# Softmax division in PSUM before a three-pass output projection, expert outputs scattered per tile, layer norms scaled on ScalarE

## What is computed

```python
x = layernorm(x + ttt(x))          # L0: chunked test-time-training "attention", 8 chunks of 256
x = layernorm(x + relu_moe(x))     # L0: router, top-1 of 8 experts with a capacity, 128->512->128
x = layernorm(x + attention(x))    # L1: 16 heads of 64, softmax(Q K^T / 8) V, then Wo and a bias
x = layernorm(x + gated_moe(x))    # L1: gate sigmoid(top logit), 8 experts 128->352->128, and a shared one
```

## Time and profile before

| | us |
|---|---|
| median of 3 runs (lowest, highest) | 1915.83 (1913.63, 1916.16) |
| the profiled execution's own time | 1917.79 |
| its span in the profile | 1916.5 |
| PE busy of the span | 1685.4 (88%) |
| VectorE busy | 1327.3 (69%) |
| POOL busy | 1286.8 (67%) |
| ScalarE busy | 787.4 (41%) |

### The profile page before, as it was taken

How to read it: one execution, slowest core, us unless ns; L and a number is a source line. 1 busy time by engine, 2 the same in 40 slices (tenths; PEclk the granted TensorE clock), 3 DMA queues, 4 the chain that set the end, 5 groups by cost and what they waited for, 6 DMA issues and landing times.

```text
span 1916.5 us, 34532 instructions
## 1 busy us (share of the span) xinstructions
PE 1685.4 (88%) x13785; PEld 986.1 (51%) x13785; DVE 1327.3 (69%) x2083; ACT 787.4 (41%) x1183; POOL 1286.8 (67%) x652
## 2 busy tenths in 40 slices
PE   4988851848999999999999999999999999995793
PEld 3766641825555555555555555555555545442483
DVE  3566545666777777777777777777777788764575
ACT  3455430523444444444444444444444444442221
POOL 2233303135988888888888888888888889894303
PEclk8677755969999999999999999999999999997797
DMA  7000000210000000000000000000000000002112
GB/s 237 3 3 3 4 1 20 62 28 1 1 1 1 1 1 1 1 1 1 1 1 1 1 1 1 1 1 1 1 1 1 1 1 1 1 1 81 49 42 61
DMA packets 35190, 29.70 MB, mean 15 GB/s; under 512 B 4060, under 2 KB 30928, under 8 KB 35032
## 3 DMA queue, kind: packets, MB, share of 16 engines
q1 hardware_dynamic: 27064, 20.28, 3.5%
q0 software_dynamic: 2048, 4.20, 0.7%
q10 hardware_dynamic: 5920, 3.01, 0.5%
HBM read 18.31 MB, written 9.18 MB: 14 GB/s over the span
## 4 chain that ended last, share of the span: by engine, by line
PE 68%; DVE 8%; issue 6%; POOL 3%; DMA 1%; ACT 1%; DVEq 0%; POOLq 0%
PE psum L1799 22%; PE psum L1784 16%; PE psum L1759 9%; PE psum L1781 6%; DVE a_On L1994 3%; DVE a_mx L1962 3%; PE psum L1431 2%; PE psum L1813 2%; PE psum L1807 2%; PE psum L1732 1%; PE psum L1392 1%; PE psum L1207 1%; PE psum L1219 1%; PE psum L1441 1%; PE psum L1733 1%
## 5 line engine op out<-in xcount | busy, mean ns | idle before, releaser
L2075 POOL TENSOR_TENSOR a_acc<-a_acc,a_Pb 128x1024 f32<-128x1024 f32 x448 | 1066.0, 2379 | 147.0 <-ACT a_Pb L1899 102.0
L1962 DVE TENSOR_REDUCE a_mx<-psum 128x2 f32<-128x1024 f32 x512 | 624.9, 1223 | 274.7 <-PE psum L1759 274.2
L1899 ACT ACTIVATE a_Pb<-psum 128x1024 f32<-128x1024 f32 x512 | 498.1, 1024 | 646.5 <-PE psum L1784 646.5
L1799 PE MATMUL psum<-a_Pb,a_Vb 128*64 128x512 f32 x2048 | 494.1, 603 | 0.0
L1799 PEld LDWEIGHTS psum<-a_Pb,a_Vb 128*64 128x64 f32 x2048 | 127.0, 136 | 242.5 <-issue 171.8
L1759 PE MATMUL psum<-a_Kh,a_Qh 64*128 64x512 f32 x1024 | 237.3, 457 | 15.5 <-DVE a_mx L1962 15.0
L1759 PEld LDWEIGHTS psum<-a_Kh,a_Qh 64*128 64x128 f32 x1024 | 99.2, 184 | 251.9 <-issue 243.2
L1781 PE MATMUL psum<-a_Mr,a_ones_r 64*128 64x512 f32 x1024 | 203.8, 393 | 0.0
L1784 PE MATMUL psum<-a_Qh,a_Kh 64*128 64x512 f32 x1024 | 202.9, 391 | 0.0
L1784 PE MATMUL psum<-a_Ql,a_Kh 64*128 64x512 f32 x1024 | 202.8, 391 | 0.0
L1784 PE MATMUL psum<-a_Qh,a_Kl 64*128 64x512 f32 x1024 | 202.3, 389 | 0.0
(11 more groups left out here) (372 smaller groups left out, 1905.1 us busy)
## 6 DMA issues: line engine op xcount, KB each, us to landing
x_rows<-zero ACTq DMA_DIRECT2D x2, 1472.0 KB, 15.7
g_w<-in_L_ffn_w_eDF_dram SPq DMA_DIRECT2D x2, 1408.0 KB, 8.8
r_W<-in_L_ffn_W_dram SPq DMA_DIRECT2D x1, 2048.0 KB, 11.5
r_tile_x<-x_rows SPq DMA_DIRECT2D x23, 64.0 KB, 1.9
y_rows<-r_tile_y SPq DMA_DIRECT2D x23, 64.0 KB, 1.5
g_tile_x<-x_rows SPq DMA_DIRECT2D x23, 64.0 KB, 1.9
y_rows<-g_tile_y SPq DMA_DIRECT2D x23, 64.0 KB, 1.5
g_w<-in_L_ffn_w_eFD_dram SPq DMA_DIRECT2D x2, 512.0 KB, 10.8
```

The source lines that it names most:

```text
L1799: last = pe.matmul(ps[HEAD[h], B_O, :], b.Vb[:, p // 2 % 2, kc, at], b.Pb[:, step % BUFS, h * QT:(h + 1) * QT], start=(kc == 0), stop=(kc ...
L1899: act.activation(b.Pb[:, step % BUFS, :], ps[:, slot:slot + 2, :].rearrange("p a b -> p (a b)"), ACT.Exp, scale=SCALE).then_inc(S["probs"], 1)
L1962: v.tensor_reduce(b.mx[:, :, qc, quarter:quarter + 1], ps[:, bank:bank + 2, :], AX.X, ALU.max).then_inc(S[f"free{bank}"], 1)
L2075: g.tensor_tensor(b.acc[:, u, :], before, b.Pb[:, step % BUFS, :], ALU.add).then_inc(S["added"], 1)
```

## The change

It has five parts. (1) The division by the row sums happens in place in PSUM: two reciprocals each in rounds 2 and 3, one 128x512 multiply at the end of round 3; then ScalarE writes the rounded high part and VectorE in round 4 the low part, and the projection runs as three rounded passes like the others. `Wo` gets high and low parts (a fourth ScalarE copy and a fourth POOL subtraction ahead of the first expert layer). The output job moves from round 2 of the unit after next to round 5 of the next unit, the values job from round 3 to round 6; the mask product uses rounded operands. (2) Rows of `x_rows` get a 129th word, the token's number (a spare row's number where no token is). POOL scatters each finished tile straight to the tokens' rows of `y_rows`; four plain loads on SP replace the 16 gathers. The load of tile t+5 now waits for the scatter of tile t to have landed, since the words lie in the loaded tile; there are five buffers. (3) The norms' scaling is four ScalarE activations per group, with VectorE's work on the next group written ahead. (4) The zero fill's source is a memset of 23 rows per partition, made by POOL after its constants; loads of attention weights wait for the fill. (5) The second router's product waits for all five small loads of its layer instead of one.

```diff
+    pool.did(g.iota(k.i32[3][:, :], pattern=[[P, NT + SLOTS_T]], base=0, channel_multiplier=1))
+    g.tensor_copy(k.x_pad[:, :, P:P + 1].bitcast(I32), k.i32[3][:, 0:NT].unsqueeze(2)).then_inc(S["const"], 1)
+    pool.did(g.memset(rows, 0.0))
+    g.tensor_copy(rows[:, :, P:P + 1].bitcast(I32), k.i32[3][:, NT:].unsqueeze(2)).then_inc(S["const"], 1)
...
-    a.wait_ge(S["const"], 1)
+    a.wait_ge(S["const"], 2)
...
+    def scales(g):
+        v.wait_ge(S["deviations"], 4 * stage + g + 1)
+        dve.did(v.reciprocal(k.sd[:, at], k.sd[:, at]))
+        v.scalar_tensor_tensor(k.shift[:, at], k.mv[:, at, 0:1].rearrange("p a b -> p (a b)"), -1.0, k.sd[:, at],
+                               ALU.mult, ALU.mult).then_inc(S["norm_scales"], 1)
+    for g in range(4):
+        moments(g)
+        if g:
+            scales(g - 1)
+    scales(3)
...
+        for i in range(g * GROUP, (g + 1) * GROUP):
+            last = act.activation(k.x_all[:, i, :], k.y_all[:, i, :], ACT.Identity, bias=k.shift[:, i:i + 1], scale=k.sd[:, i:i + 1])
...
+def tile_rows_back_pool(k, r, b):
+    for t in range(SLOTS_T):
+        u = t % BUFS_T
+        g.wait_ge(S["tile_yt"], SLOTS_T * r + t + 1)
+        g.wait_ge(S[f"tile_x{u}"], 16 * tile_uses(r, t))
+        place = b.xt[:, u, P:P + 1].bitcast(U32)
+        g.indirect_dma_start(k.y_rows[r], bass.IndirectOffsetOnAxis(place, 0), b.yt[:, u, :], None).then_inc(S[f"tile_y{u}"], 16)
+def outputs_sp(k, r, got):
+    stores_done(sp, k, r)
+    for g in range(4):
+        rows = k.y_rows[r][at.start * P:at.stop * P, :].rearrange("(a p) d -> p a d", p=P)
+        sp.dma_start(got[:, at, 0:P], rows).then_inc(S[f"tokens_out{g}"], 16)
...
-BUFS_T = 4
+BUFS_T = 5
...
-        sp.wait_ge(S["tile_in"], SLOTS_T * r + t - BUFS_T + 1)
+        sp.wait_ge(S[f"tile_y{u}"], 16 * (tile_uses(r, t) - 1))
...
-    if d == 2 and U > 1:
-        return "out", U - 2
-    if d == 3 and p // 2 < PAIRS // 2 - 1:
-        return "v", p // 2 + 1, U % RN
     if d == 4 and U < UNITS - 2:
         return "q", U + 2
+    if d == 5 and U:
+        return "out", U - 1
+    if d == 6 and p // 2 < PAIRS // 2 - 1:
+        return "v", p // 2 + 1, U % RN
...
+        pe.matmul(ps[:, bank, :], hi, b.Onh[:, :], start=True, stop=False)
+        pe.matmul(ps[:, bank, :], lo, b.Onh[:, :], start=False, stop=False)
+        end(pe.matmul(ps[:, bank, :], hi, b.Onl[:, :], start=False, stop=True), bank)
...
-        if U and 2 <= d <= 5:
-            invert(U - 1, d - 2)
+        if U and d in (2, 3):
+            for part in (2 * d - 4, 2 * d - 3):
+                invert(U - 1, part)
+        if U and d == 4:
+            normalised_low(U - 1)
         if early:
             maximum(*early[1:])
...
-        if U and d in (3, 5, 6, 7):
-            normalise(U - 1, (3, 5, 6, 7).index(d))
+        if U and d == 3:
+            normalise(U - 1)
```

More of the change, by code:

```diff
@@ L841, in ttt_pool, with norms_dve @@
         residual(c)
-def norm_dve(k, n, g, have_stats=False):
+def norms_dve(k, stage, residual=None):
     S, v, dve = k.S, k.nc.vector, k.dve
-    tiles, at = range(g * GROUP, (g + 1) * GROUP), slice(g * GROUP, (g + 1) * GROUP)
-    if not have_stats:
-        for i in tiles:
[L850 to L860, removed]
@@ L863, in norm_act, with moments @@
-def norm_act(k, n, g):
-    S, act = k.S, k.nc.scalar
-    at = slice(g * GROUP, (g + 1) * GROUP)
-    act.wait_ge(S["variances"], n + 1)
-    act.activation(k.sd[:, at], k.mv[:, at, 1:2].rearrange("p a b -> p (a b)"), ACT.Sqrt, bias=k.eps[:, 1:2]).then_inc(S["deviations"], 1)
+    def moments(g):
+        tiles = range(g * GROUP, (g + 1) * GROUP)
+        if residual:
+            residual(g)
+            for i in tiles:
+                dve.did(v.bn_stats(k.stats[:, i, :], k.y_all[:, i, :]))
+        dve.wait()
+        for i in tiles:
+            last = v.bn_aggr(k.mv[:, i, :], k.stats[:, i, :])
+        last.then_inc(S["variances"], 1)
@@ L1226, in relu_act @@
     b, S, ps, act = k.r, k.S, k.ps, k.nc.scalar
-    for g in range(4):
-        norm_act(k, g, g)
+    norms_act(k, 0)
     transpose_route_act(k, 0, b.route_xT)
@@ L1253, in relu_dve @@
     b, S, ps, v, dve = k.r, k.S, k.ps, k.nc.vector, k.dve
-    for g in range(4):
-        norm_dve(k, g, g, True)
+    norms_dve(k, 0)
     v.wait_ge(S["relu_turned"], 1)
@@ L1329 @@
 QT = 512
-GW_LOADS = (1, 4, 5)
+GW_SHARED, GW_ROUTED = 5, 5
 def allocate_gated(k, mem):
@@ L1638, in __init__ @@
                 self.job(misc_job(R), B_P)
-        for key in (("out", UNITS - 2), ("sum", UNITS - 1), ("out", UNITS - 1)):
+        for key in (("sum", UNITS - 1), ("out", UNITS - 1)):
             self.job(key, B_P)
@@ L1810, in output @@
     def output(U):
-        pe.wait_ge(S["normalised"], 4 * U + 4)
+        freed(("sum", U))
         bank = begin(("out", U))
-        end(pe.matmul(ps[:, bank, :], k.att_o[:, U // NU, :], b.On[:, :], start=True, stop=True), bank)
+        hi, lo = (w[:, U // NU * P:(U // NU + 1) * P] for w in k.att_o)
+        pe.matmul(ps[:, bank, :], hi, b.Onh[:, :], start=True, stop=False)
+        pe.matmul(ps[:, bank, :], lo, b.Onh[:, :], start=False, stop=False)
+        end(pe.matmul(ps[:, bank, :], hi, b.Onl[:, :], start=False, stop=True), bank)
     def misc(key):
@@ L1855, in attention_pe @@
     weigh(ROUNDS - 1)
-    output(UNITS - 2)
     sums(UNITS - 1)
@@ L1925, in attention_act @@
             {"q": queries, "k": keys, "v": values}[key[0]](*key[1:])
-        if key and key[0] == "sum":
-            sums(U - 1)
         if d == 0 and U:
             heads_out(U - 1)
+        if d == 3 and U:
+            normalised(U - 1)
     heads_out(UNITS - 1)
-    sums(UNITS - 1)
-    for g in range(4):
-        norm_act(k, 8 + g, g)
+    normalised(UNITS - 1)
+    norms_act(k, 2)
 def attention_dve(k):
@@ L2052, in attention_norm_dve, with residual @@
     S, ps, v, dve = k.S, k.ps, k.nc.vector, k.dve
-    for g in range(NU):
+    def residual(g):
         at = slice(GROUP * g, GROUP * g + GROUP)
```

178 lines of the change are left out of this document (95 added, 83 removed).

## The result

The changed kernel takes **1891.76 us** in the median of four runs (1887.10 to 1896.85), the kernel before 1915.99 beside it: ratio 0.988, 95% interval 0.986 to 0.990. It is 24 us faster, 1.3%. Forecast were 1900.8 us, a range of 1875 to 1922, and a chance of 0.8 for faster. The profiled execution of the changed kernel is its quickest run, 1887.1 us, with a span of 1885.9; a part of the 30.6 us between the two spans is therefore this run's luck, and experiment e7 shows where that part lies.

A forecast was written before the change was run, and what follows sets the result against it. PE was taken as the main bound, with POOL's adds the next floor in attention. Attention -5.5, first layer +2, second -5, norms -3 and -1.5, start -2 sum to -15 from 1915.8: 1900.8 us, range 1875 to 1922.

The forecast's parts named there:

- Round 7, round 0 and the output projection: Attention: PE's waits behind the old multiply vanish and the projection shortens; 0.8, 0.25 and 0.16 us gained a unit.
- The paired reciprocals: Attention rounds 2 and 3: second reciprocal delays the early maximum, PE waits 0.55 us in each; 1.1 lost a unit.
- Reciprocals in PSUM: Attention division: each taken at 0.94 us, as in SBUF; rival of dearer ones, 0.26 a unit, 1909 us, chance 0.1.
- If the pairs are hidden, a unit falls by 1.1: Rival in attention: the maxima don't hold PE; 33 us less over 30 units, 1868 us, chance 0.08.
- The ring: Expert tiles: load-to-scatter round trip of 7.4 us per three tiles, 2.46 us a tile; +10 first layer, +5 second.
- rival of a shorter ring: Expert tiles: POOL starts its scatter 0.3 us after the wait, 6 us less, 1894 us; counted within the forecast's 0.6.
- rival in which PE cools: Expert tiles: slower ring lowers PE's clock, 3.1 us a tile, 20 us more, 1921 us; chance 0.12.
- Descriptors behind VectorE's copies: Expert tiles, rival: POOL's descriptors wait for VectorE's weight copies, up to 0.8 us a ring, 1912 us; chance 0.1.
- Gathers to plain loads: End of each expert layer: plain loads shorten the way from last tile's output to last scaling, 27.4 to 17.3 us; -10.1.
- The fourth subtraction: First expert layer: POOL's extra weight subtraction holds a VectorE copy once more; +2 us.
- Norms: Ahead of the routers: scaling on ScalarE frees VectorE; -3 us at the first router, -1.5 at the second.
- Start: Kernel start: the later zero fill lets PE's first product start earlier; -2 us, bounds 4 earlier and 4 later.

The follow-up runs named there:

- e7: The changed kernel run and profiled again, with no edit, as a control; 1895.24 us.
- e1: Changed kernel with its four reciprocals a unit spread over rounds 1 to 3, no longer paired ahead of an early maximum; 1875.65 us, ratio 0.980 to the kernel before.
- e8: Changed kernel with the sum copied to SBUF by ScalarE, paired reciprocals SBUF to SBUF, multiply with two SBUF operands; 1911.48 us, ratio 0.997 to the kernel before.
- e11: Changed kernel with all four reciprocals of a unit in round 2, ahead of its early maximum; 1940.9 us in a single run.
- e2: Changed kernel with six tile buffers instead of five, some semaphores shared with earlier stages; 1878.11 us, ratio 0.981 to the kernel before.
- e3: Changed kernel with four tile buffers instead of five; 1946.24 us in a single run.
- e5: Kernel before with only the attention part of the change, stores, gathers and norms as before; 1894.75 us, ratio 0.988 to the kernel before.

## Why the prediction was right, and where it was wrong

The forecast was 9 us above the median, inside the range, and faster, as forecast. Part by part:

- **Round 7, round 0 and the output projection** (0.8, 0.25 and 0.16 gained): right in their sum, as the next point shows, and round 7 by itself: 4.62 us, forecast 4.6.
- **The paired reciprocals** ("1.1 lost" a unit): the mechanism was right, the size wrong, and this is the step that failed. The term was computed as 1.69 + 0.92 + 0.92 and a maximum of 1.23; measured were 1.68 for the pair and 1.16 for the maximum, so each of the two rounds waits 0.29 and not 0.55. That is 0.52 a unit. The forecast's -0.1 a unit becomes -0.62, and a unit fell from 40.84 to 40.19. In the six units from the 24th, -0.5 becomes -1.02, and they fell from 40.4 to 39.3 and from 39.5 to 38.45. The same 0.52 in 28 units is the 15 us by which attention was missed. e1 checks the new size: with the pairs taken apart, rounds 2 and 3 last 4.38 and a unit 39.62, 0.57 less.
- **Reciprocals in PSUM**: the lower bound taken, 0.94, was nearly right. One at a time they take 953 ns in the mean in PSUM (e1) and 942 in SBUF (before); in pairs the medians are 904 in PSUM and 896 in SBUF (e8). The Trainium skill, page "VectorE: DVE Perf Modes", section on the TRN2 errata, lists 120 fixed cycles for a PSUM source against 58 for an SBUF one, by estimate 65 ns more; that did not show here.
- **"If the pairs are hidden, a unit falls by 1.1"** (rival, 0.08): the maxima do hold PE, e1 and e11 show it from both sides; but hidden they give 0.58 a unit, the 16 us of e1.
- **The ring** (2.46 us a tile): right in its length, its division by three and both layers' totals, and e2 and e3 bear it out at four and six buffers. One of its parts was wrong: POOL starts 0.27 after the release, not 0.75. The ring as a whole came out no shorter, so the rival of a shorter ring is not borne out. The rival in which PE cools is nearly out: in the first profile the clock was 1.00 from 345 us to the last turn of the first layer, as before the change. In e7 it was 0.66 from 358 to 363 us (0.91 from 352 to 370), and the turns took 3.2 us longer, far from the rival's 20. The argument given against it, a busy share well above half, is borne out by no row: the earlier trace rows has a reduced clock where PE is busy 75%. With four buffers, 3.9 us a tile, the clock of the second layer's tiles was 0.88 (1835 to 1919 us), and e3 came out 7 above its sum.
- **Descriptors behind VectorE's copies** (rival): POOL's scatters of tiles take 996 ns in the mean in the first layer and 957 in the second, the gathers before 947. That is at most 0.05 a ring and not 0.8. Out.
- **Gathers to plain loads** (-10.1 in each layer): right, -10.5 and -10.6.
- **The fourth subtraction** (+2): it held a copy of VectorE for 2.37 us in the first tiles, and e5, which has it but no ring, needs 43.8 us for the first layer's turns against 42.0. Right.
- **Norms** (-3 and -1.5): -1.6 ahead of the first router, where ScalarE's four scalings take 1.65 us of a group's 1.7 to 1.9 and not 1.4 with the root; -2.8 ahead of the second, where e5, without the new norms, already has 1.2 of it (91.0 against 92.2); and at the end of the kernel a loss of 1.6, which stands inside the -10.6.
- **Start** (-2): wrong. It costs 4.3. The bound was named ("4 later if the fill's 516-byte rows hold ScalarE longer"), and the value between the bounds was chosen by the earlier PE product alone, without asking which engine is the last to be ready for the next step. That the profiled pair shows -1.7 is the accident that e7 uncovers: in the first profile PE's clock happened to rise 33 us earlier than in the second.

So the right total comes of two misses that partly cancel, 15 us too little from attention and some 4 to 6 too much from the start (4.3 slower at the learning rates, 2.4 in the mean at the first root, against a forecast of 2 faster). The other terms stand by their landmarks, within the few us by which two profiles differ. That the sum came out in the range is in part luck: of its 15 us it gave 3.5 to attention with the fourth subtraction and 11.5 to the rest, and e5 got 22 from the first alone, while the rest, from e5 to e7, gave nothing that the runs can tell.

## What to carry to other kernels

Ask of a buffer ring what its round trip is and how many buffers the pipeline itself keeps: the round trip over what is left is the pace, and one more buffer may be worth more than the change that made the ring. Put instructions that another engine's next step doesn't wait for behind those that it does wait for, one at a time; by their place alone the same four reciprocals cost 16 us more (the change) or 65 more (e11) than in e1. And when an experiment gives the expected number, look for the rows that were to make it: in e8 they were not there.

## What was not expected of the hardware

- A multiply on VectorE with two SBUF operands took 1429 ns beside POOL's adds, with one of them in PSUM 684, for the same 512 columns. In the last unit, with no add running, the same two SBUF operands took 699. Which operands an instruction has, and what runs beside it, can matter more than its elements.
- Reciprocals of 128 columns: 942 ns in the mean one at a time, but two back to back take 1.68 us from the first's start to the next instruction's.
- The issue of a fill of two tables of 1.5 MB holds the issuing engine's own stream: 4.45 us with rows of 512 bytes from one tile of zeros, 11.62 with rows of 516 bytes from a tile for each, 16.49 on SyncE beside the loads. Which of the two differences, row length or source, makes it longer was not tried.
- Two executions of one program were alike to 0.05 us for 55.6 us, and then PE's clock rose at 55.9 us in one and at 89.3 in the other: the same four products took 0.61 and 1.02 us. The clock column shows 1.00 for both, since ahead of the first clock record it shows 1.00 whatever PE does; durations of equal products (272 or 421 ns) tell the level there.
